# GpSimd makes three of four low parts in a projection, with a shorter routing, later waits for stores, and an output merged into the attention

## The chip, the cores and the metric

The kernel runs on one core of a Trainium2 chip. The metric is the device time of one execution in microseconds (us), the median over runs. Engine names: TensorE (PE in the rows, PEld for its weight loads), VectorE (DVE), ScalarE (ACT), GpSimd (POOL), SyncE (SP, which here only issues DMAs). A "q" behind an engine's name is its instruction queue.

## The reference

The input x has shape (2, 2048, 256). With `xn = layernorm(x)` over the last axis, the output is `x + attention(xn) + experts(xn)`:

```
qkv = xn @ Wqkv;  q, k, v of 16 heads of 16
q, k = rope(q), rope(k)                      # pairs of neighbours rotated by position
attn = softmax(causal(q @ k.T / 4));  attention = (attn @ v) @ Wout + bout

p = softmax(xn @ gate_w.T + gate_b)          # 10 gates: 8 experts and 2 null ones
weights, selected = top_k(p, 2)              # a null expert's weight is dropped, the rest rescaled
experts = sum over the selected e < 8 of  weight_e * (xn @ expert_w[e] + expert_b[e])
```

## The kernel before

The 4096 rows are 32 tiles of 128. The program has three blocks: `project`, `attend` and `output`. Between two blocks every engine waits until all engines have come to the end of the block. Within a block each engine has a list of instructions written out by hand, which it follows in order; semaphores tie them together. `wait_ge` stops the engine that meets it, and all that is queued behind.

**project** runs eight steps, s = 2j + b, each for 4 tiles (512 rows) of batch b. A step normalises rows (`norm_a` and `norm_c` on VectorE, `deviation` and `normal_x` on ScalarE, two steps ahead), turns them on TensorE (`transposes`), splits them in an fp16 high part (`high_x`, ScalarE) and low part (`low_x`, VectorE), and multiplies them by the weights: `queries` 0 to 3 give queries and keys transposed in psQ, `values` gives values and gate logits in psV. A product of split numbers is three fp16 products, high by high, high by low, low by high.

A query or key of index k (0 to 3) goes this way: `rope(s, k)` on VectorE (L559) multiplies psQ by cosines and sines into `turn[k]`; GpSimd combines two indices at once (L356 subtracts, L358 adds; `rot[k]` is the result); ScalarE writes the fp16 high part (`high`, L413, into `part[k]`); the low part `rot - high` is made by GpSimd for k = 0 and 2 (`low`, L345) and by VectorE for k = 1 and 3 (`split`, L564); and SyncE stores `part[k]` to memory (L250, semaphore `part_stored[k]`). `high(s, k)` waits until the store of step s-1 has landed, since it writes over the same tile. SyncE's order in a step is: normalised rows (L257), values (L245, once `copy_v` on ScalarE, L395, has filled `vst`), parts 0 to 3, and one expert's weights (L261), which `high_e` (ScalarE) and `low_e` (VectorE, L583) split, one expert a step.

Behind the steps comes the routing, almost all on VectorE (L633 to L700), each instruction waiting for the one before: add the gate bias, subtract the row's maximum, find the first and the second gate (`largest`, five instructions each), and write `sent`, which says for each row and expert whether the row goes there (L661). TensorE counts rows by expert (32 products, L771) and ranks them within each expert (33 products, L773 and L775). VectorE rounds the counts up to tiles of 128, a product sums them (L778), and VectorE works out each row's place `idx`, and `etab`, the expert of each of the 76 tiles (L695 to L700). ScalarE meanwhile issues the loads of the first group's keys and queries (L74), 24 DMAs. At the end SyncE waits for all stores and these loads.

**attend** goes through 8 groups of 4 heads in an order written out by hand. It begins with items for the first group (`first_items`): products of queries and keys (L1463, L1466) of which VectorE takes maxima (L1306). All semaphores of the block begin at one, which GpSimd sets, one instruction each, in the order in which they were made:

```python
for every in sems:
    pool.sem_inc(every, PV0 if every is pv_ok else ONE)
```

The expert products of 72 tiles run between the attention's, and behind the last group's scores TensorE does 7 and then 14 products that nobody reads (`idle_products`), and normalises the last outputs through psP.

**output** turns the attention's result for each of 32 tiles (L1673), copies it (ScalarE, L1694), multiplies it by Wout (L1684), adds the experts' part and the product to `acc` (VectorE, L1700 and L1704), and stores it.

## Time and profile before

| | us |
|---|---|
| median of 3 runs | 989.14 (989.03 to 990.25) |
| profiled execution, own time | 994.68 |
| its span (first to last instruction) | 993.0 |
| `project` | 0 to 133.5 |
| `attend` | 133.8 to 954.6 |
| `output` | 954.9 to 993.0 |

Over the span TensorE is busy 902.7 us (91%), VectorE 837.9 (84%), ScalarE 737.8 (74%), GpSimd 463.2 (47%), and the mean granted clock is 0.969. Busy time is a mean over stages with different limits; each stage must be read by itself. A row of the order of time gives start, duration, engine, line, operation, written tile and read tiles, shapes and, in brackets, how long the engine had been idle and what released it. Where a row merges several instructions (x2), its duration is that from the first's start to the last's end.

### The profile page before, as it was taken

Reading aid. Unit: us, or ns where it says so; the run is one execution under the profiler, and the core shown is the slowest. Engines: PE = TensorE matmul, PEld = TensorE weight load, DVE = VectorE, ACT = ScalarE, POOL = GpSimd, SP = SyncE. Lnnn points to the kernel's source line nnn. Section 1 sums busy time; section 2 is a strip of 40 time slices with the busy share of each in tenths; the row PEclk is TensorE's granted clock in tenths of the full one; section 3 lists DMA queues with packets and bytes.
Section 4 is the critical chain, followed back from the end, with each engine's and each line's share of the span. In section 5 each row is a group of like instructions: output and inputs, shape, how many; then the busy total and the mean of one; then the engine's idle time right before and its main releaser. Section 6 shows DMA issues by size and latency. Waiting matters only on the chain. (4 is left out here: it accounts for less than half of the span.)

```text
span 993.0 us, 22231 instructions
## 1 busy us (share of the span) xinstructions
PE 902.7 (91%) x7911; PEld 395.2 (40%) x7911; DVE 837.9 (84%) x1112; ACT 737.8 (74%) x1556; POOL 463.2 (47%) x588
## 2 busy tenths in 40 slices
PE   2888457999999999999999999999999999999888
PEld 1544233232432344444443544353444333322267
DVE  5999879999899978987889788978888899894856
ACT  3566323788788888888888789878887888789822
POOL 4677748585200353344834574355142344355620
PEclk9999775999999999999999999999999999999989
DMA  9777820301200424345414542265334321122113
GB/s 323 265 257 252 281 73 22 97 3 41 68 2 2 118 81 124 87 131 149 129 55 117 151 147 69 77 170 139 66 90 126 97 59 50 34 58 67 39 53 128
DMA packets 82133, 106.65 MB, mean 107 GB/s; under 512 B 10048, under 2 KB 59112, under 8 KB 81000
## 3 DMA queue, kind: packets, MB, share of 16 engines
q1 hardware_dynamic: 74536, 85.83, 27.2%
q0 software_dynamic: 6528, 17.83, 7.3%
q10 hardware_dynamic: 960, 1.57, 0.5%
q8 instruction: 64, 1.05, 0.4%
q14 instruction: 45, 0.37, 0.1%
HBM read 67.37 MB, written 37.50 MB: 106 GB/s over the span
## 5 line engine op out<-in xcount | busy, mean ns | idle before, releaser
L1306 DVE TENSOR_REDUCE blk<-psP 128x2 f32<-128x1024 f32 (+2 forms) x560 | 623.1, 1159 | 91.4 <-PE psP L1466 46.6
L1239 ACT ACTIVATE probs<-psS 128x512 f32<-128x512 f32 (+3 forms) x1280 | 588.0, 540 | 101.8 <-PE psS L1521 96.0
L1521 PE MATMUL psS<-Qs,Ks 50*128 50x512 f16 (+3 forms) x1280 | 329.1, 352 | 11.5 <-ACT probs L1239 7.0
L1463 PE MATMUL psP<-Ks,Qs 48*128 48x512 f16 (+2 forms) x1264 | 294.3, 359 | 22.6 <-DVE blk L1306 9.1
L1583 PE MATMUL psO<-probs,Vs 128*32 128x512 f32 (+3 forms) x2560 | 299.3, 545 | 6.0 <-POOL probs L1139 4.9
L1139 POOL TENSOR_SCALAR_AFFINE_SELECT probs<-probs 128x512 f32<-128x512 f32 x128 | 88.3, 690 | 337.6 <-ACT probs L1239 301.3
L1521 PEld LDWEIGHTS psS<-Qs,Ks 50*128 50x128 f16 x1280 | 96.0, 93 | 240.5 <-ACT probs L1239 155.2
L1463 PEld LDWEIGHTS psP<-Ks,Qs 48*128 48x128 f16 x1264 | 79.9, 94 | 119.6 <-DVE blk L1306 77.1
L1466 PE MATMUL psP<-later,eye 64*128 64x128 bf16 x1024 | 103.7, 222 | 0.0
L1583 PEld LDWEIGHTS psO<-probs,Vs 128*32 128x32 f32 x2560 | 52.8, 108 | 85.8 <-issue 65.1
L1466 PEld LDWEIGHTS psP<-later,eye 64*128 64x128 bf16 x1024 | 78.5, 99 | 19.9 <-issue 2.2
L1161 POOL DMA_INDIRECT xn<-norm_scratch,ids x72 | 69.4, 964 | 20.6 <-issue 8.1
L1556 PE MATMUL psS<-xn 128*128 128x256 f16 x432 | 57.0, 272 | 2.1 <-DMA xn<-be_scratch 0.8
L717 PE MATMUL psQ<-xp,wqp 128*128 128x512 f16 x192 | 47.6, 395 | 10.5 <-DVE turn L559 5.9
L1153 POOL TENSOR_SCALAR xn<-lane,at 128x128 f16<-128x128 f32 x64 | 39.7, 621 | 36.6 <-issue 19.6
L1556 PEld LDWEIGHTS psS<-xn 128*128 128x128 f16 x432 | 39.7, 97 | 18.1 <-issue 12.2
L1148 POOL DMA_INDIRECT xn<-expert_scratch,idx x32 | 30.3, 946 | 28.6 <-ACT probs L1239 25.9
L1173 POOL TENSOR_TENSOR xn<-xn 128x512 f16<-128x512 f32 x36 | 41.7, 1157 | 3.0
L1260 ACT COPY xn<-psS 128x512 f32<-128x512 f32 x36 | 21.1, 586 | 27.2 <-PE psS L1558 27.2
L1156 POOL TENSOR_SCALAR xn<-lane,at,number 128x76 f16<-128x76 f32 x64 | 40.6, 634 | 0.0
L559 DVE TENSOR_TENSOR turn<-psQ,trig 128x1024 f32<-128x1024 f32 x32 | 38.4, 1218 | 2.6 <-DVE part L564 1.8
L1256 ACT COPY xn<-psS 128x1024 f16<-128x1024 f16 x36 | 37.1, 1032 | 1.3 <-PE psS L1540 0.7
(186 smaller groups left out, 770.2 us busy)
## 6 DMA issues: line engine op xcount, KB each, us to landing
xn<-we_scratch SPq DMA_DIRECT2D x72, 256.0 KB
expert_scratch<-xn SPq DMA_DIRECT2D x36, 256.0 KB, 3.4
v_scratch<-vst SPq DMA_DIRECT2D x8, 1024.0 KB, 4.0
qk_scratch<-part SPq DMA_DIRECT2D x32, 256.0 KB, 4.0
Vs<-v_scratch SPq DMA_DIRECT2D x16, 512.0 KB, 3.9
Qs<-qk_scratch SPq DMA_DIRECT2D x168, 32.0 KB
Ks<-qk_scratch SPq DMA_DIRECT2D x168, 32.0 KB
acc<-x SPq DMA_DIRECT2D x8, 512.0 KB, 9.4
```

Of the source, the lines that this page charges most:

```text
L717: ins = pe.matmul(out, lhs(x, w, k), rhs(x, w, k), start=(n == 0), stop=(n == len(todo) - 1))
L1139: nc.gpsimd.affine_select(out=v, in_=v, compare_op=ALU.is_ge, fill=0.0, base=0, pattern=[[0, HG], [1, P]], channel_multiplier=-1).then_inc ...
L1156: nc.gpsimd.tensor_scalar(at_tile[:, n, :], lane[:, 0:MTILES], at[:, 0, n:n + 1], number[:, t:t + 1], ALU.is_equal, ALU.mult).then_inc(lis ...
L1161: nc.gpsimd.indirect_dma_start(out=xt[n % 2][:, t, :], out_offset=None, in_=xd[:, :], in_offset=bass.IndirectOffsetOnAxis(ap=ids[:, 2 * n ...
L1173: nc.gpsimd.tensor_tensor(xs[n % 2][:, 1, :], rows, xs[n % 2][:, 0, :], ALU.subtract).then_inc(x_split, 1)
L1239: nc.scalar.activation(probs[u % NPR][:, h, q0:CH], psS[:, k % SB, q0:CH], ACT.Exp, scale=exp_scale).then_inc(s_read[k % SB], 1)
L1306: nc.vector.tensor_reduce(out, src, AX.X, ALU.max).then_inc(item_ok[slot], 1)
L1463: ins = pe.matmul(psP[:, slot, at:at + w], Qs[r][rows, qt // CT, p, t * P:(t + 1) * P], Ks[r][rows, kc, p, 0:w], start=True, stop=True)
L1466: ins = pe.matmul(psP[:, slot, at + w - P:at + w], eye[all_rows, i, :], later[all_rows, i, :], start=False, stop=True, skip_group_check=True)
L1521: pe.matmul(psS[:, k % SB, q0:CH], Ks[r][rows, kt // CT, p, kt % CT * P:(kt % CT + 1) * P], Qs[r][rows, c, p, q0:CH], start=True, stop=Tru ...
L1556: pe.matmul(psS[:, bank, t * D:(t + 1) * D], xT[buf][:, w0, at_k:at_k + P], wt[2 * buf + t][:, of:of + D], start=(n == 0), stop=False)
L1583: ins = pe.matmul(psO[h * VW:(h + 1) * VW, q0:CH], Vs[r][:, kt, h * VW:(h + 1) * VW], probs[u % NPR][:, h, q0:CH], start=(kt == 0), stop=e ...
```

## The change

In `project`, GpSimd makes the low part of index 1 as well in each step; in the last step it makes all four, and the low parts of the last two experts. ScalarE no longer does `high` of index 2 and 3 at the start of the next step but in its own, behind `normal_x`. VectorE's `norm_a` and `low_e` move within the step. In the last step TensorE does `values` ahead of `queries` 2 and 3. The routing has fewer and smaller instructions: the first gate is found from the already subtracted maximum, counting goes by blocks of four tiles, counts are summed on VectorE, and `etab` is worked out as one column of 128 partitions and turned by a trip through memory. The waits for the last step's stores move into `attend`, and the buffers that these stores read lie where `attend` has `Qs[1]` and `Ks[1]`, which it writes only behind these waits. GpSimd sets `item_ok` first. `output` is merged into `attend`, without a block's end between them, in the same PSUM tiles, and the idle products are gone. The queries of the first group are loaded by SyncE instead of ScalarE.

```diff
+                if s == LAST:
+
+                    for k in range(QKT):
+                        sp.wait_ge(part_stored[k], ONE + 16 * LAST)
+                    load_heads(sp, qk_s, Qs[0], 0, Q_PARTS, slice(0, CHUNKS), 0, ahead_in)
                 for k in range(QKT):
                     sp.wait_ge(split_ok[k], ONE + s + 1)
...
-                    sp.wait_ge(el_ok, ONE + e + 1)
-                    sp.dma_start(we_s[e], wep[e % 2][:, :, :, :].rearrange("p w k n -> p (w k n)")
-                                 ).then_inc(e_stored[e % 2], 16)
+                    for late in {LAST - 1: (), LAST: (LAST - 1, LAST)}.get(e, (e,)):
+                        sp.wait_ge(el_ok, ONE + late + 1)
+                        sp.dma_start(we_s[late], wep[late % 2][:, :, :, :].rearrange("p w k n -> p (w k n)")
+                                     ).then_inc(e_stored[late % 2], 16)
+            sp.wait_ge(be_ok, ONE + 1)
+            sp.dma_start(be_s.rearrange("e p d -> e (p d)"), be_p[:, :, :].rearrange("e p d -> e (p d)")).then_inc(be_stored, 16)
             for b in range(2):
                 sp.wait_ge(v_stored[b], ONE + 16 * CHUNKS)
-                sp.wait_ge(e_stored[b], ONE + 16 * EXPERTS // 2)
-            for k in range(QKT):
-                sp.wait_ge(part_stored[k], ONE + 16 * NB * CHUNKS)
-            sp.wait_ge(be_ok, ONE + 1)
-            sp.dma_start(be_s.rearrange("e p d -> e (p d)"), be_p[:, :, :].rearrange("e p d -> e (p d)")).then_inc(spare, 16)
             sp.wait_ge(ahead_in, ONE + 16 * 2 * LOADS)
...
                         low(s, k0)
+                        if k0 == 0 or s == LAST:
+                            low(s, k0 + 1)
+                        if s == LAST:
+                            low_e(LAST - 1 + k0 // 2)
+
+            def low_e(e):
+                pool.wait_ge(eh_ok, ONE + e + 1)
+                nc.gpsimd.tensor_tensor(wep[e % 2][:, 1, :, :], we_sb[:, :, e * D:(e + 1) * D], wep[e % 2][:, 0, :, :],
+                                        ALU.subtract).then_inc(el_ok, 1)
...
+                ins = nc.scalar.activation(wep[e % 2][:, 0, :, :], we_sb[:, :, e * D:(e + 1) * D], ACT.Copy,
+                                           scale=wscale[:, OF_E:OF_E + 1])
+                if e >= LAST - 1:
+
+                    ins.then_inc(whole_ok, 1)
+                    act.wait_ge(whole_ok, ONE + e - LAST + 2)
+                    ins = nc.scalar.activation(we_sb[:, :, e * D:(e + 1) * D], we_sb[:, :, e * D:(e + 1) * D], ACT.Copy,
+                                               scale=wscale[:, OF_E:OF_E + 1])
+                ins.then_inc(eh_ok, 1)
...
-                    if not first:
-                        high(s - 1, 2)
-                        high(s - 1, 3)
                     if more:
                         high_x(s + 1, 1 - b)
                     high(s, 0)
                     if not last:
                         deviation(s + 2, b)
                     high(s, 1)
-                    copy_v(s, j, b)
                     if not last:
                         normal_x(s + 2, j + 1, b)
-                    high_e(s)
+                    if more:
+                        high(s, 2)
+                        copy_v(s, j, b)
+                        high(s, 3)
+                        high_e(s)
+                    else:
+                        copy_v(s, j, b)
+                        high_e(s)
+                        high(s, 2)
+                        high(s, 3)
 
             for j in range(CHUNKS):
                 body(j, j == 0, j == CHUNKS - 1)
-            high(LAST, 2)
-            high(LAST, 3)
             act.wait_ge(gate_in, ONE + 1)
...
                     rope(s, j, 1)
                     if not first:
                         split(s - 1, 3)
+                    if not last and not first:
+                        dve.wait_ge(x_in[s + 2], 16)
+                        norm_a(s + 2, j + 1, b)
                     if first:
                         scale_e()
                     if more:
                         low_x(s + 1, 1 - b)
                     rope(s, j, 2)
-                    if not first:
-                        low_e(s - 1)
-                    if not last:
+                    if first:
                         dve.wait_ge(x_in[s + 2], 16)
                         norm_a(s + 2, j + 1, b)
-                    rope(s, j, 3)
+                        rope(s, j, 3)
                     if not last:
                         norm_c(s + 2, b)
-                    split(s, 1)
+                    if not first:
+                        rope(s, j, 3)
+                        if s < LAST:
+                            low_e(s - 1)
...
-            low_e(LAST)
...
-            split(LAST, 3)
...
+            step(nc.vector.scalar_tensor_tensor(out=hot[0][:, :, :], in0=lg[:, :, :], scalar=0.0, in1=row(lower[:, :]),
+                                                op0=ALU.is_ge, op1=ALU.mult))
+            stepped()
+            foremost(hot[0][:, :, :])
...
+            dve.wait_ge(sent_ok, ONE + 1)
+            with nc.allow_low_precision(reason="counts up to 32 are whole numbers"):
+                nc.vector.tensor_reduce(some[:, :, :], sent[:, 0:TILES, :].rearrange("p (b t) e -> p b e t", t=BLOCK), AX.X,
+                                        ALU.add).then_inc(blocks_ok, 1)
+                dve.wait_ge(blocks_ok, ONE + 1)
+                nc.vector.tensor_reduce(total[:, :], some[:, :, :].rearrange("p b e -> p e b"), AX.X, ALU.add
+                                        ).then_inc(blocks_ok, 1)
+            none = (gm, gr)
+            for i in range(2):
+                step(nc.vector.tensor_tensor(none[i][:, :], hot[i][:, :, EXPERTS], hot[i][:, :, EXPERTS + 1], ALU.add))
+
             dve.wait_ge(count_ps, ONE + 1)
...
+            step(nc.vector.tensor_copy(countf[:, :], count[:, :]))
+            stepped()
+            step(nc.vector.tensor_tensor(shares[:, :, :], upto[:, :, :, :].rearrange("p i e f -> p (i e) f"),
+                                         countf[:, :].unsqueeze(1).to_broadcast([P, 2 * EXPERTS, EXPERTS]), ALU.mult))
+            stepped()
+            step(nc.vector.tensor_reduce(first[:, :, :].rearrange("p i e -> p (i e)"), shares[:, :, :], AX.X, ALU.add))
...
+            step(nc.vector.tensor_scalar(past[:, :], first[:, 1, :], row0[:, 0:1], None, ALU.is_le))
+            stepped()
+            step(nc.vector.tensor_reduce(number_past[:, :], past[:, :], AX.X, ALU.add))
+            stepped()
+            step(nc.vector.tensor_scalar_min(eplace[:, :], number_past[:, :], float(EXPERTS - 1)))
...
+                    if s == LAST:
+                        values(s, b)
...
+            pe.matmul(rank, upper[:, :], flat[:, 0:width], start=True, stop=True)
+            for t in range(1, BLOCK):
+                pe.matmul(inside[:, :, t * EXPERTS:BLOCK * EXPERTS], full[:, :], blocks[:, :, 0:(BLOCK - t) * EXPERTS],
+                          start=False, stop=True, skip_group_check=True)
+            pe.wait_ge(blocks_ok, ONE + 2)
+            pe.matmul(psV[:, 1, 0:EXPERTS], full[:, :], total[:, :], start=True, stop=True).then_inc(count_ps, 1)
+            for n in range(1, BLOCKS):
+                ins = pe.matmul(rank[:, n * BLOCK * EXPERTS:width].rearrange("p (b t e) -> p b t e", t=BLOCK, e=EXPERTS), full[:, :],
+                                some[:, 0:BLOCKS - n, :].unsqueeze(2).to_broadcast([P, BLOCKS - n, BLOCK, EXPERTS]),
+                                start=False, stop=True, skip_group_check=True)
+            ins.then_inc(ahead_ps, 1)
...
+            rows_of_ones(0)
             load_v(0, 0, 0)
             load_v(0, 0, 1)
+            for k in range(QKT):
+                sp.wait_ge(part_stored[k], ONE + 16 * B * CHUNKS)
+            for b in range(2):
+                sp.wait_ge(e_stored[b], ONE + 16 * EXPERTS // 2)
+            sp.wait_ge(be_stored, ONE + 16)
+            rows_of_ones(1)
+            sp.dma_start(et_s, eplace[0:MTILES, :]).then_inc(et_out, 16)
             n = first_items.index(("m", 1, 3))
             store_m(n % 2, n // 2, 0, 0, 3)
             load(1, 1, 1)
             load(1, 1, 0)
+            sp.wait_ge(et_out, 16)
+            sp.dma_start(etab[:, :], et_s.rearrange("n o -> o n")).then_inc(et_in, 16)
             sp.dma_start(wo[:, :, :], wout.rearrange("(k p) n -> p k n", p=P)).then_inc(wo_in, 16)
...
-            for every in sems:
+            for every in item_ok + [x for x in sems if x not in item_ok]:
...
+            for t in range(TILES):
+                act.wait_ge(t_ps, t + 1)
+                if t >= 2:
+
+                    act.wait_ge(o_ps, t - 1)
+                nc.scalar.copy(aT[t % 2][:, :, :].rearrange("p k n -> p (k n)"), psS[:, t % SB, 0:D]).then_inc(t_ok, 1)
...
+            dve.wait_ge(y_in[1], 16 * TILES)
+            dve.wait_ge(added, ONE + TILES)
+            for t in range(TILES):
+
+                nc.vector.scalar_tensor_tensor(out=acc[:, t, :], in0=second(t), scalar=wsel[:, 1, t:t + 1],
+                                               in1=acc[:, t, :], op0=ALU.mult, op1=ALU.add).then_inc(y_add, 1)
+                dve.wait_ge(o_ps, t + 1)
+                dve.wait_ge(y_add, t + 1)
+                nc.vector.tensor_tensor(acc[:, t, :], out_place(t), acc[:, t, :], ALU.add).then_inc(o_add, 1)
...
-                                idle_products(7)
+                                turn_out(0)
+                                turn_out(1)
...
-            idle_products(14)
...
+            pe.wait_ge(wo_in, ONE + 16)
             for t in range(TILES):
-                if t + 1 < TILES:
-                    turn(t + 1)
+                if t + 2 < TILES:
+                    turn_out(t + 2)
                 pe.wait_ge(t_ok, t + 1)
-                if t >= 4:
+                if t in (0, 2):
+                    slot = out_slot(t)
+                    pe.wait_ge(item_ok[slot], ONE + (ITEMS - slot + 1) // 2)
+                elif t >= 4:
                     pe.wait_ge(o_add, t - 3)
                 for k in range(KC):
-                    ins = pe.matmul(ps[:, t % 4, 0:D], aT[t % 2][:, k, :], wo[:, k, :], start=(k == 0), stop=(k == KC - 1))
+                    ins = pe.matmul(out_place(t), aT[t % 2][:, k, :], wo[:, k, :], start=(k == 0), stop=(k == KC - 1))
                 ins.then_inc(o_ps, 1)
```

## Rows read from the trace of the kernel before

**Rows 1.** Table of stretches: us, busy us of each engine (instructions), granted clock, DMA share, GB/s.

```profile
60.00:80.00 20.00, 16.70 (x106) 10.06 (x105) 19.55 (x37) 11.30 (x25) 14.53 (x11) 1.00 0.72 256
...
200.00:940.00 740.00, 720.15 (x6731) 289.51 (x6729) 631.69 (x732) 624.95 (x1326) 324.11 (x416) 1.00 0.30 85
```

**Rows 2.** VectorE in order of time, one step of the projection (s = 3).

```profile
59.27 2.35 DVE L559 TENSOR_TENSOR turn<-psQ,trig 128x1024 f32<-128x1024 f32 x2 [0.25 <-DVE part L564]
...
64.76 0.74 DVE L583 SCALAR_TENSOR_TENSOR wep<-we_sb,wscale,wep 128x512 f16<-128x512 f32 x1
...
68.63 1.79 DVE L564 TENSOR_TENSOR part<-turn,part 128x512 f16<-128x512 f32 x1
70.67 2.36 DVE L559 TENSOR_TENSOR turn<-psQ,trig 128x1024 f32<-128x1024 f32 x2 [0.25 <-DVE part L564]
```

**Rows 3.** GpSimd in order of time, same step.

```profile
68.60 1.27 POOL L356 TENSOR_TENSOR turn<-turn 128x512 f32<-128x512 f32 x1 [2.09 <-DVE turn L559]
...
72.21 1.16 POOL L345 TENSOR_TENSOR part<-turn,part 128x512 f16<-128x512 f32 x1 [0.66 <-ACT part L413]
```

**Rows 4.** ScalarE and SyncE in order of time; last, the view of line L250.

```profile
33.67 1.07 ACT L395 ACTIVATE vst<-psV 128x512 f32<-128x512 f32 x2
...
63.66 0.62 ACT L413 CAST part<-turn 128x512 f16<-128x512 f32 x1 [1.45 <-POOL turn L356]
...
67.89 1.08 ACT L395 ACTIVATE vst<-psV 128x512 f32<-128x512 f32 x2
...
68.99 0.33 SPq L245 DMA_DIRECT2D v_scratch<-vst  x1
69.37 4.94 SPq L250 DMA_DIRECT2D qk_scratch<-part  x4
...
106.85 0.62 ACT L413 CAST part<-turn 128x512 f16<-128x512 f32 x1 [2.38 <-DMA qk_scratch<-part]
...
DMA to landing us min/median/max: 2.2/4.0/5.4
```

**Rows 5.** Order of time, routing; last, SyncE's waits of 98 to 175 us.

```profile
109.36 0.20 ACT L398 ACTIVATE lg<-psV 128x40 f32<-128x40 f32 x1
...
111.71 1.54 DVE L633 TENSOR_TENSOR lg<-lg,gb_sb 128x320 f32<-128x320 f32 x1
...
115.36 5.62 ACTq L74 DMA_DIRECT2D Ks<-qk_scratch  x11
...
118.54 0.49 DVE L656 SCALAR_TENSOR_TENSOR gq<-hot,lg 128x320 f32<-128x320 f32 x1
...
121.68 0.43 DVE L661 TENSOR_TENSOR sent<-hot 128x256 bf16<-128x256 f32 x1
...
125.54 0.28 DVE L665 TENSOR_SCALAR count<-psV 8x128 uint32<-8x128 f32 x1 [3.44 <-PE psV L771]
...
127.96 0.42 DVE L677 TENSOR_TENSOR lg<-psV,first 128x256 f32<-128x256 f32 x1
...
131.53 0.78 DVE L695 TENSOR_TENSOR past<-first,row 128x608 f32<-128x608 f32 x1
...
133.17 0.20 DVE L700 TENSOR_SCALAR etab<-row 128x76 uint32<-128x76 f32 x1
...
SPq L84 <- DMA Qs<-qk_scratch: 3.4, 1, 3.4
```

**Rows 6.** The attention's first instructions in order of time; last, a stretch.

```profile
136.26 0.29 PE L1463 MATMUL psP<-Ks,Qs 48*128 48x128 f16 x1 [8.55 <-POOLq L1133]
...
137.32 0.69 DVE L1306 TENSOR_REDUCE blk<-psP 128x4 f32<-128x512 f32 x1 [2.33 <-PE psP L1466]
...
172.00:176.00 4.00, 4.00 (x29) 1.58 (x27) 1.95 (x3) 2.02 (x4) 2.26 (x4) 0.50 0.29 79
```

**Rows 7.** VectorE and TensorE in order of time, at the output's begin.

```profile
953.62 0.42 DVE L1329 TENSOR_TENSOR on<-psP,rs 128x256 f32<-128x256 f32 x1
...
955.80 1.13 PE L1684 MATMUL ps<-wo,aT 128*128 128x256 f32 x4 [0.24 <-ACT aT L1694]
```

189 lines of the change are left out of this document (76 added, 113 removed).

## The prediction

> **What bounds the kernel now.** I read the table of stretches first. The attention stage, 200 to 940 us, has TensorE busy 720 of 740 us, and no line of its loops changes. The projection (60 to 80 us) has VectorE busy 19.55 of 20 us, TensorE 16.7, GpSimd 14.5, and DMA at 0.72 of its capacity [rows 1]. So I look for gains at three seams: the projection with its routing tail (up to 133.4 us), the first microseconds of the attention, and the output.
>
> VectorE's order of time shows one step of the projection: the first rotation starts at 59.27 and that of the next step at 70.67, a pitch of 11.40, with 0.25 idle in it [rows 2]. VectorE sets the pitch, and the low part of index 1 at its end (68.63) takes 1.79.
>
> **The low part that moves.** With it VectorE loses everything from 68.63 to 70.67, 2.04 us, and its own work is 9.36 a step [rows 2]. The row is mostly waiting: GpSimd's sum starts at 68.60 and takes 1.27, and the low part ends about 0.55 after that [rows 2, 3]. GpSimd pays 1.16 for the same low part [rows 3], and goes to some 8.6 us a step with four sums at 1.27 and three low parts: no bound by itself. [...]
>
> **The new loop.** ScalarE now does the third high part and the value copy behind the four normalisations. The value copy (L395) therefore ends late, SyncE issues the value store after it, and the stores of the four parts stand behind that store in one queue. The high part of index 0 of the next step waits for its store to land. Before there was slack (at 63.66 ScalarE had waited 1.45 us for GpSimd), except once, at 106.85, where it had waited 2.38 us for that landing [rows 4]. The loop, by rows: value store issued at 68.99, just behind the copy, first part's store at 69.37, landing 4.0 later (the median), so 4.4 from the copy's end; high part 0.62; two low parts on GpSimd 2.3; one sum 1.27; high part of index 2, 0.62; value copy 1.08 [rows 3, 4]. That is 10.3. [...] The deviation, and the rotation behind it, also hang on that high part. [...]
>
> **Where that leaves the logits.** In step 0 the value copy ended at 34.7 [rows 4]; behind 2.07 of normalising and a high part with its sum it ends at about 37.9. Steps 1 to 5 at 10.9 bring it to 92.4, where five at 11.4 brought it to 91.8. Before, the two last steps were short, as they have nothing to normalise; now they still hang on the store: copy 6 at 103.3; then landing 4.7, two high parts 1.3, copy 1.1, logits 0.2: 110.7. Before, the logits were copied at 109.56 [rows 5]. They come 1.1 late, but VectorE no longer has the two last expert low parts and adds the bias at 110.7 and not at 111.71. So eight steps of a lighter VectorE are worth 1.0 us.
>
> **Routing, first part.** From 111.71 to the end of L661 at 122.11 are 10.40 us [rows 5]. Gone are the low part of index 3 (0.6) and two gate instructions; an undisturbed one has a pitch of 0.52 (118.54 and its 0.49 [rows 5]): 1.7 less. Against this, GpSimd still has some seven long instructions to do (a low part, two sums, two low parts, two expert low parts), where it had about three. Each VectorE instruction with two SBUF inputs may wait for the one under way: the first one did, 1.54 instead of 0.5 [rows 5]. Bounds: nothing, or 1.2 for each of six; I take 0.6 each, 3.6, since half of an instruction is the mean wait. The sent table then ends at 110.7 + 10.4 - 1.7 + 3.6 = 123.0.
>
> **Routing, the rest.** From 122.11 to 127.96 were 5.85: VectorE waited 3.44 for 32 counting products, converted, and waited for a product behind 32 others [rows 5]. Now: two sums over tiles (0.45 and 0.25), one product (0.25), three small instructions (0.2 each), a product and a sum of 128 elements (0.3 each): 2.4 with the hops. These sizes are not in the trace; the bounds are 1.8 and 3.2 by the 0.2 of L700 and the 0.42 of L677 [rows 5]. The seven block products (896 columns) run under them: the 32 narrow ones before, some 4,200 columns, took about 2 us. From 127.96 to 133.37 were 5.41; the table of experts (131.53 to 133.17, 1.64 for two instructions on 608 elements) falls to 0.4, and two additions leave: 1.5 less, 3.9. VectorE ends the projection at 123.0 + 2.4 + 3.9 = 129.3 in place of 133.4: minus 4.1.
>
> **Does anything else hold the exit?** The waits for stores of the last step move into the attention. SyncE still waits for the first head loads. ScalarE's first 12 stood at 114.79 to 120.98 and the other 12 behind them, with 3.4 of waiting for the landing [rows 5]. Now SyncE issues the query half before the last parts' stores, and ScalarE the key half after its last high part. I put that at 118 and the exponential at 119.5; 5.7 of issuing and 3.4 of landing end at 128.6. Hidden, but by 0.7 only: a faster routing would be held there.
>
> **The attention's first item.** TensorE's first product starts at 136.26, held by GpSimd's counters, of which the one it needs is about the thirtieth; VectorE's first maximum waits 2.33 and starts at 137.32 [rows 6]. With that counter first, TensorE is done by the time VectorE's own counter, then the thirtieth, is raised: 136.3. Minus 1.05. From there to 163 VectorE is the full engine, so its earlier start carries through. [...] The expert table's trip through memory is two small transfers on SyncE's queue, some 1 us before a store that comes behind 24 loads and for which nobody waits at once; nothing.
>
> **Output.** The last normalisation ends at 954.04 and the one before it 0.62 earlier, at 953.42; the first output product starts at 955.80, behind 14 idle products, the exit and one transpose with its copy [rows 7]. Now transposes and copies of the first tiles run while VectorE normalises: first product at 953.46, and one tile's transposes (0.22) fewer behind it. Minus 2.55. TensorE still does 32 tiles of 1.09, so nothing more comes out of it.
>
> **Sum.** 4.1 + 1.05 + 2.55 = 7.7. The profiled execution took 994.68 for a span of 993.0, and would take 987.0; the median of the three runs, 989.14, is 5.5 below the profiled one, and I take the same difference from it: 981.4.
>
> **Rivals.**
> A, the store loop is worse than the step it replaces: for it speaks the wait at 106.85 [rows 4], against it a DMA share of 0.72 [rows 1], under 0.8 at the new pitch. With a landing of 5.4 instead of 4.4 the step is 11.9: six steps give 6 us back, 987.4; if only half of the landings are that late, 984.5.
> B, the loop is looser (expert low part never in the way, landing hidden): pitch 9.9, six steps 6 us sooner, and the loads shift with them: 975.5. For it speaks that VectorE's work is 9.36; against it the single queue.
> C, routing is stretched by GpSimd as far as it can be: every one of six waits 1.2, as at 68.63 [rows 2, 3]: 3.6 more, 985. [...] At the other end no contention at all is 3.6 less, but the key loads hold 2.9 of it: 980.7.
> D, slower: the same queue, with the value store so late that each step costs more than 12.5. Then 6 x 1.6 = 9.6 eats all 7.7 and the 2 us of a measurement. [...] At 13 a step: 6 x 2.1 = 12.6, less 7.7, gives 994.
> E, no change: the attention gives back what the stages ahead of it gain, by a later rise of its clock: 988 to 990. Against it: the output's part lies behind the attention.
>
> **Numbers.** The forecast, 978.5 to 984, has 0.50; A 0.17; B 0.17; C (the stretched end) 0.07; D 0.04; E 0.05. A measurement of this kernel tells a change of about 0.2%, 2 us, from none. Faster by more than that needs less than 987.2: the forecast, B, C and most of A, 0.90; the same 0.06; slower 0.04. The range that leaves out 0.2 reaches half of B and most of A: 974.5 to 986.8.
>
> **What would show it.** The pitch of the first rotation (11.40) between 10.3 and 11.2; ScalarE's high part of index 0 released by a DMA in each step, and not by GpSimd; low parts of VectorE only for index 3; the write of `sent` ending near 123, with instructions of 0.8 to 1.5 among those with two inputs; exit at 129.3; the first maximum 2.4 after the attention's begin instead of 3.5; output products 0.04 after the normalisation. I am wrong if the pitch is 9.4 or above 11.4, if the key loads end the stage, or if the clock's rise, at 176 before, moves by more than the stages do.

## The result: no gain, and 0.2% lost

The changed kernel took 992.02 us (median of 14 runs, 987.51 to 994.08); the kernel before, run beside it, 989.58 (14 runs, 988.63 to 991.33). The ratio is 1.0021, 95% interval 1.0012 to 1.0031. Forecast were 981.4, with 974.5 to 986.8 as the range and 0.04 for slower.

The profiled execution took 994.08 for a span of 992.3. The table of stretches of the changed kernel, beside [rows 1]:

```profile
60.00:80.00 20.00, 16.64 (x98) 10.30 (x97) 15.67 (x33) 12.03 (x26) 14.84 (x12) 0.91 0.76 274
200.00:940.00 740.00, 718.85 (x6726) 290.21 (x6722) 628.47 (x721) 621.78 (x1318) 320.43 (x416) 1.00 0.30 85
```

VectorE is busy 15.67 of 20 us, no longer 19.55: the work did leave it. The steps didn't get shorter for it. The granted clock is 0.91 and no longer 1.00: it is at its lower level, 0.50, from 71.3 to 74.7 us, behind 3.3 us in which TensorE was busy for 1.04.

What holds a step stands in ScalarE's, GpSimd's and SyncE's order of time, one step of the changed kernel and the begin of the next (compare [rows 2 to 4]). In the changed kernel L250 is the value store, L260 the part stores, L430 `high` and L353 `low`:

```profile
85.19 0.33 SPq L250 DMA_DIRECT2D v_scratch<-vst  x1
85.56 4.34 SPq L260 DMA_DIRECT2D qk_scratch<-part  x4
...
91.72 0.62 ACT L430 CAST part<-turn 128x512 f16<-128x512 f32 x1 [4.38 <-DMA qk_scratch<-part]
...
92.41 2.27 POOL L353 TENSOR_TENSOR part<-turn,part 128x512 f16<-128x512 f32 x2 [3.57 <-ACT part L430]
...
98.17 0.33 SPq L250 DMA_DIRECT2D v_scratch<-vst  x1
98.54 4.01 SPq L260 DMA_DIRECT2D qk_scratch<-part  x4
...
102.97 0.62 ACT L430 CAST part<-turn 128x512 f16<-128x512 f32 x1 [2.65 <-DMA qk_scratch<-part]
```

The loop is the forecast one: value store (85.19), landing of part 0, high part of index 0 (91.72), and 6.45 later the next value store (98.17). Its landing wasn't the 4.4 of the forecast: from value store to high part are 6.53 in this step and 4.80 in the next (98.17 to 102.97). The view of waits from 24 to 117 us sums it up:

```profile
ACT part L430 <- DMA qk_scratch<-part: 22.0, 8, 4.4
POOL part L353 <- ACT part L430: 18.5, 9, 3.6
```

In each of the seven steps after the first, ScalarE waits for the landing of part 0 (the eighth wait of the row, 0.16, is for part 1); the kernel before did so once [rows 4]. The first rotation of the steps starts at 25.95, 35.43, 47.22, 58.54, 71.04, 82.31, 95.30 and 106.46; before, at 25.78, 36.45, 47.88, 59.27, 70.67, 82.08, 93.48 and 101.79. From 47.22 on the pitch is 11.2 to 11.3 and 12.5 to 13.0 in turns. In five of the seven steps high part 0 starts 4.8 after the value store's issue, in two later: 6.05 (at 67.46) and 6.53 (at 91.72).

The end of the projection in order of time, with the queues of SyncE and ScalarE (L74 are the first head loads), answers to [rows 5, 6]:

```profile
116.81 6.12 SPq L74 DMA_DIRECT2D Qs<-qk_scratch  x12
117.50 0.84 DVE L662 TENSOR_TENSOR lg<-lg,gb_sb 128x320 f32<-128x320 f32 x1
...
122.96 3.41 ACTq L74 DMA_DIRECT2D Ks<-qk_scratch  x9
122.97 2.01 SPq L260 DMA_DIRECT2D qk_scratch<-part  x4
...
127.42 0.50 DVE L692 TENSOR_TENSOR sent<-hot 128x256 bf16<-128x256 f32 x1
...
134.31 0.15 DVE L742 TENSOR_SCALAR eplace<-number_past 128x1 uint32<-128x1 f32 x1
138.95 0.48 DVE L1420 MEMSET ones<- 128x512 f16 x1 [4.49 <-PEq L84]
...
141.05 2.69 DVE L1393 TENSOR_REDUCE blk<-psP 128x4 f32<-128x512 f32 x3 [0.95 <-POOLq L1213]
```

and this is the line of SyncE's waits there:

```profile
SPq L278 <- DMA Ks<-qk_scratch: 8.1, 1, 8.1
```

Routing starts 5.8 late (117.50, before 111.71), but VectorE ends only 1.1 late (134.46, before 133.37). Then it stands for 4.49, because SyncE waits for the head loads: their last issue ends at 126.37, and the attention begins at 138.95, where the kernel before began at 133.83.

### The profile page after: what moved, and what is told of

It reads as the page before. It is cut to its first block, busy times and chain, and to the rows that moved or that the text cites. A ratio compares the mean times of both kernels' runs of the same rounds, so it can differ in the third digit from the quotient of the medians.

```text
span 992.3 us, 22081 instructions
## 1 busy us (share of the span) xinstructions
PE 901.6 (91%) x7836; PEld 393.1 (40%) x7836; DVE 826.4 (83%) x1102; ACT 740.1 (75%) x1558; POOL 465.0 (47%) x599
## 3 DMA queue, kind: packets, MB, share of 16 engines
q8 instruction: 64, 1.05, 0.4%
## 4 chain that ended last, share of the span: by engine, by line
PE 56%; DVE 19%; ACT 5%; issue 3%; POOL 2%; DMA 1%; SPq 1%; POOLq 0%; ACTq 0%; DVEq 0%
PE psO L1683 20%; DVE blk L1393 15%; PE psS L1618 13%; PE psP L1560 8%; ACT probs L1319 5%; PE psS L1653 4%; PE psP L1563 3%; PE psP L1752 3%; PE psS L1637 2%; DVE acc L1501 1%; PE psP L1733 1%; DVE xn L1401 1%; DMA xn<-be_scratch 1%; PE psS L1655 1%; PE psS L1664 1%
## 5 line engine op out<-in xcount | busy, mean ns | idle before, releaser
L1219 POOL TENSOR_SCALAR_AFFINE_SELECT probs<-probs 128x512 f32<-128x512 f32 x128 | 82.0, 641 | 341.2 <-ACT probs L1319 305.0
L430 ACT CAST part<-turn 128x512 f16<-128x512 f32 x32 | 19.8, 617 | 33.4 <-DMA qk_scratch<-part 22.0
```

The lines of the kernel that those rows point to most:

```text
L1219: nc.gpsimd.affine_select(out=v, in_=v, compare_op=ALU.is_ge, fill=0.0, base=0, pattern=[[0, HG], [1, P]], channel_multiplier=-1).then_inc ...
```

## Experiments

Each is the changed kernel with the edit shown, if it isn't said otherwise. The kernels g, k, l, m, n, p and q also have two lines near the end of the program, called the pauses here and told in the last part of this section; m and q are therefore read beside k, the changed kernel with the pauses alone, and n and p beside g. "Third memset" is the write of `nmp`, 0.72 after the attention's first instruction on VectorE; where an expectation speaks of the first memset with 128.6 or 139.7, it is this third one. Times from the traces, us:

```
kernel                         routing begins  VectorE's last  third memset
before                              111.71         133.17         134.55
changed kernel                      117.50         134.31         139.67
a, order undone                     111.88         127.27         132.38
b, order alone                      118.05         141.01         142.39
c, parts 0 and 1 first              108.30         124.76         128.56
d, key loads ahead                  117.22         133.76         145.03
g, c with the pauses                108.22         124.67         129.61
k, changed with the pauses          116.59         134.07         139.76
m, values copied early              111.94         129.42         135.62
n, c and m together                 105.78         123.26         129.16
q, queries loaded early             116.32         133.79         135.13
p, n and early queries              105.76         123.23         126.13
```

**Which half costs?** a_order_undone gives the old order back to the four engines:

```diff
-                        if k0 == 0 or s == LAST:
-                            low(s, k0 + 1)
...
+                    if not first:
+                        high(s - 1, 2)
+                        high(s - 1, 3)
...
+                    split(s, 1)
```

> The changed kernel with the projection's order of work put back to that of the kernel before (GpSimd makes low parts 0 and 2, VectorE 1 and 3, ScalarE makes high parts 2 and 3 at the next step's begin, values after queries in the last step); the routing, the stores' waits and the merged output stay. Theory 1 (the new order lost the time): the steps are 11.4 us again, the routing begins near 111.7 (changed kernel 117.50) and takes the changed kernel's 17.0 us, so VectorE is done near 129; the key loads, issued from 115 on, land by about 130; the attention's begin is near 130 where the kernel before had 133.8 and the changed one 138.95. With 1.4 us from the first item and 1.3 from the output that is 989.6 - 4.1 - 2.7 = 983 us (981 to 986). Rival 1 (the loads end the stage wherever VectorE is): the begin stays at 133.8, 987 us. Rival 2 (the order is innocent, the waits moved into the attention or the merged output cost it): 991 to 993 us.

Measured: 982.06, ratio 0.9925 (0.9901 to 0.9949). b_order_alone puts the new order, and nothing else, into the kernel before (the same lines with signs changed).

> The kernel before with only the new order of the projection (three low parts on GpSimd, ScalarE's new order, VectorE's new order, values ahead of the last queries, the last expert low parts on GpSimd); routing, waits and output are those of the kernel before. Theory 1 (the new order's loop through the value store and the landing of part 0 sets the step at 11.3 and 12.5 to 13 us in turns): routing begins 5.8 us late, at 117.5, and everything after it is as late: 989.6 + 5.8 = 995.4 us (993.5 to 997). Rival (the steps are longer only together with the moved waits or loads): 989 to 991 us.

Measured: 996.34, ratio 1.0067 (1.0040 to 1.0095). So the order costs 7.1 us and the rest gains 7.2: theory 1 both times, by the totals. Inside a, VectorE was done earlier than expected (127.4 for 129) and the attention began later (third memset 132.38 for some 130): it lies 5.1 behind VectorE's last instruction, not 1.4 as before. That is the loads' part, below.

**Is it the landing?** c_parts_first moves two stores in one queue:

```diff
+                store_parts((0, 1))
                 sp.wait_ge(v_ok, ONE + 2 * s + 2)
                 sp.dma_start(v_s[...], vst[b]...)
...
-                for k in range(QKT):
+                store_parts((2, 3))
```

> The changed kernel, but SyncE issues the stores of parts 0 and 1 of a step ahead of its value store (they are ready some 4 to 5 us before the values are copied). Theory 1 (the step is the loop value copy, stores, landing of part 0, next high part 0): the landing lies beside the value copy, ScalarE's 22 us of waits for the landing of part go, the step comes to 10.4 to 11.2 us (VectorE is busy for 10.3 of it), the routing begins near 110.5 to 112, VectorE ends near 128, the key loads some 4 us behind it, near 132: 992.0 - 6.5 = 985.5 us (983 to 988). Rival 1 (the DMA queues' throughput holds the step: 2 MB a step leave in one burst): the wait moves to another store, steps near 12, 991 to 993 us. Rival 2 (GpSimd's longer sums and low parts hold it): steps 11.4 to 12, 989 to 992 us.

Measured: 981.92, ratio 0.9916 (0.9888 to 0.9945). No run lies near that median: four took 977.92 to 979.56, four 984.27 to 985.99 (two groups of runs, told below). With the pauses, which leave one group, it is 979.64 (g) against 991.41 (k): 11.8 us less. That is more than the 4 to 9 us expected. The table of stretches, and from the view of waits, what is left of the landing's up to 100 us:

```profile
60.00:80.00 20.00, 16.98 (x106) 10.04 (x105) 17.89 (x36) 13.29 (x29) 17.10 (x14) 1.00 0.75 268
```

```profile
ACT part L434 <- DMA qk_scratch<-part: 1.1, 1, 1.1
```

The engines do the same work in the same order as in the changed kernel; only the place of two stores differs. The rotations come every 10.76 us (35.41 to 89.23, five steps), the clock is 1.00 again, and routing starts 9.2 earlier. The same bytes go out in 1.1 us less a step, so throughput didn't hold the step of the changed kernel. i_old_order_parts_first is the control, the same edit under the old order:

> The changed kernel with the projection's old order of work (as in a_order_undone), and parts 0 and 1 stored ahead of the values. A control. Theory 1 (the part stores' place matters only in the new order, where the high part of the next step waits for their landing): VectorE sets the step at 11.40 us as before and nothing changes against a_order_undone: 981 to 983 us in the lower group of runs. Rival (the earlier stores help any order, through less crowded queues): 978 to 980 us.

Measured: 987.66 (985.65 to 988.63; all its runs are of the upper of the two groups), and not the 981 to 983 expected of the lower one. Group for group it is the same: profiled span 986.6 where a_order_undone, also in its upper group, had 986.2, routing at 111.89 as against 111.88. No effect: the stores' place matters only where something waits for it.

m_copy_early attacks the other leg of the loop, in the changed kernel (with the pauses):

```diff
+                    if more:
+                        copy_v(s, j, b)
                     if not last:
                         normal_x(s + 2, j + 1, b)
                     if more:
                         high(s, 2)
-                        copy_v(s, j, b)
```

> The changed kernel (with the pauses), but ScalarE copies the values directly behind high part 1, as in the kernel before, ahead of the rows' normalisation and of high part 2. The part stores stay behind the value store. Theory 1 (the loop is: landing of part 0, high part 0, value copy, value store, part stores): from the release of high part 0 to the value store 3 us instead of 6.5, with the landing's 4.8 to 6.5 some 8 to 9.5 us, under VectorE's 10.3 busy us a step, so the step is 10.5 to 10.9 us and the begin of the routing 108 to 110: 979 to 982 us. Rival 1 (the queues hold the step, whatever the copy's place): 12 us steps, as k_after_gaps. Rival 2 (values copied early delay the rows' normalisation, and TensorE waits for the transposes): steps of 11.2 to 12 us, 984 to 990 us.

Measured: 988.55, ratio 0.9994 (0.9986 to 1.0003), 2.9 less than k_after_gaps. The step is 11.5 us: theory 1 is out, and so is the 12 of rival 1. It is the size of rival 2, but not for its reason: from 42 to 95 us TensorE waited only 1.2 us for normalised rows. The order of time shows another one:

```profile
53.46 0.62 ACT L430 CAST part<-turn 128x512 f16<-128x512 f32 x1 [2.85 <-DMA qk_scratch<-part]
...
54.70 1.07 ACT L412 ACTIVATE vst<-psV 128x512 f32<-128x512 f32 x2
...
57.55 0.43 SPq L267 DMA_DIRECT2D norm_scratch<-xn  x1
58.03 0.57 SPq L250 DMA_DIRECT2D v_scratch<-vst  x1
...
58.64 5.27 SPq L260 DMA_DIRECT2D qk_scratch<-part  x4
...
66.08 0.62 ACT L430 CAST part<-turn 128x512 f16<-128x512 f32 x1 [4.35 <-DMA qk_scratch<-part]
```

The values are copied by 55.8, but their store stands in SyncE's queue behind the store of the normalised rows (57.55), which waits for ScalarE's normalisation. So the value store is issued 4.57 after the high part instead of 6.45. With that 512 KB just ahead of it, part 0 is free 8.05 after it in this step and 6.2 to 6.6 in the steps between, where the changed kernel had 6.1 to 6.5 and 4.8. Most of what was won at one end of the loop was lost at the other. n_parts_first_copy_early has both edits:

> Both: parts 0 and 1 stored ahead of the values, and the values copied directly behind high part 1 (with the pauses). Theory 1: the loop is off the path already with one of the two, VectorE's chain sets 10.5 us a step, nothing is gained over g_gaps: 978 to 980 us. Rival (the loop still held a part of the step in g_gaps): steps of 10.3 us or less, 976.5 to 978 us.

Measured: 980.37, ratio 0.9909 (0.9896 to 0.9922), beside 979.64 for g_gaps (c with the pauses, below). Routing started 2.4 earlier than there (105.78, 108.22), and the attention 0.4 (129.16, 129.61). The steps had got shorter and the time hadn't, and that leads to the loads.

**The loads' end.** d_keys_ahead issues the key loads before ScalarE's last two high parts:

```diff
                         high_e(s)
+                        for k in range(QKT):
+                            act.wait_ge(part_stored[k], ONE + 16 * LAST)
+                        load_heads(act, qk_s, Ks[0], 1, K_PARTS, ...)
                         high(s, 2)
```

> The changed kernel, but ScalarE issues the twelve key loads ahead of its last two high parts, not behind the exponential: from about 117.8 us on where the changed kernel had 121.1 to 126.4, and so ahead of the last step's part stores (issued from 123.0) and the last two expert stores. Theory 1 (the key loads end the stage because they lie behind 1.5 MB of stores in the DMA engines): the loads land before VectorE is done at 134.5, the attention begins near 135 instead of 138.95: 992.0 - 3.9 = 988.1 us (987 to 989.5); the exponential is some 4 us later, near 126, and VectorE waits for it only from 128 on. Rival (the transfers share their rate whatever the order): the last load lands near 138 again, 991.5 to 992.5 us.

Measured: 1001.07, ratio 1.0094 (1.0063 to 1.0125), 9 us above the changed kernel. Not all of the 9 is the edit's: the profiled run has the slow mask told below (7.20 us), as five of the six runs seem to, and the sixth took 995.0. The edit's own part stands at the attention's begin, 5.4 later than in the changed kernel (145.03, 139.67), and that is the wrong way. Order of time, and the view of the part stores' line from 117 us on:

```profile
117.56 5.89 SPq L74 DMA_DIRECT2D Qs<-qk_scratch  x12
117.89 5.77 ACTq L74 DMA_DIRECT2D Ks<-qk_scratch  x12
123.50 5.60 SPq L260 DMA_DIRECT2D qk_scratch<-part  x4
129.14 7.43 SPq L272 DMA_DIRECT2D we_scratch<-wep  x2
136.62 0.88 SPq L275 DMA_DIRECT2D be_scratch<-be_p  x1
144.31 0.48 DVE L1420 MEMSET ones<- 128x512 f16 x1 [10.40 <-PEq L84]
```

```profile
DMA to landing us min/median/max: 19.3/20.3/20.9
```

With all 24 loads in the air together, the part stores behind them took 20 us to land, and SyncE needed 7.43 just to issue two expert stores. Between 121 and 127 us the queues moved 135 GB/s at a share of 0.67; the kernel before, whose loads followed one another on one queue, moved 174 at 0.53 over the same 6 us. The loads' 2 KB packets took some 0.18 us each here, 0.095 before and 0.13 in the changed kernel. So these packets are slower in the two kernels where two engines issue; whether that comes from the two queues or from the number of transfers in the air, these runs don't separate.

h_one_queue puts the query loads of c back behind the key loads on ScalarE:

```diff
-                    load_heads(sp, qk_s, Qs[0], 0, Q_PARTS, ...)
...
             load_heads(act, qk_s, Ks[0], 1, K_PARTS, ...)
+            load_heads(act, qk_s, Qs[0], 0, Q_PARTS, ...)
```

> The kernel with parts 0 and 1 stored first, but with the query loads issued by ScalarE behind the key loads, as the kernel before has it, not by SyncE beside them. Theory (query and key loads in the air at once slow each other: their 2 KB packets took 0.20 to 0.22 us each between 120 and 132 us of the changed kernel, 0.09 to 0.11 in the kernel before, whose 24 loads followed one another): the loads begin near 111.6 and are over 13.5 us later, as before (114.8 to 128.3), at about 125; VectorE, done at 124.8, ends the stage again and the attention's begin (first memset) moves from 128.6 to about 126.2: 2.4 us less than the kernel with parts first, some 976.5 to 978 us in its lower group of runs (that one's is 977.9 to 979.6). Rival (the issue of 24 loads on one engine takes 10 us and is as late as the crowd was): no change, 979 us.

Measured: 985.96, in the upper group; its profiled span is 982.4 where c's, in the same group, is 982.8, the third memset at 128.17 (c: 128.56). The packets did fall to 0.097, but the last ended at 126.1, as the issue of 24 loads had run to 122.9: the rival. f_queries_early is c with three of four chunks of the query loads behind the sixth step's stores:

```diff
+                    if e == LAST - 2:
...
+                        load_heads(sp, qk_s, Qs[0], 0, Q_PARTS, slice(0, CHUNKS - 1), 0, ahead_in)
```

> The kernel with parts 0 and 1 stored first, but three of four chunks of the first head group's query loads are issued by SyncE behind the stores of the sixth step (about 95 us), only the last chunk after the last value store; key loads as in the changed kernel. Theory (the loads' end, 3.8 us behind VectorE's, sets the attention's begin): most of the query bytes are in before the crowd, the rest is over by about 124, VectorE's end (124.8) sets the begin, 126.2 instead of 128.6: 2.4 us less, 976 to 977.5 us in the lower group. Rival (the loads of 6 us of issue on SyncE delay the sixth and seventh steps' stores, which delay ScalarE's high parts): the projection ends 1 to 4 us later and the gain is eaten, 978 to 982 us.

Measured: 984.48 (979.43 to 985.43). Its two lower runs took 979.4, as the lower ones of c did (977.92 to 979.56), and its profiled span is 983.0 beside 982.8: nothing won. The loads no longer held the exit (VectorE stood for 0.46), but a high part waited 3.72 for its landing at 106.87, routing began 1.0 later and VectorE ended 2.2 later: the rival again. q_after_queries_early moves them one step on, behind stores for which no later high part waits:

```diff
                     stores(e, j, b)
+                    if e == LAST - 1:
+                        for k in range(QKT):
+                            sp.wait_ge(part_stored[k], ONE + 16 * (LAST - 2))
+                        load_heads(sp, qk_s, Qs[0], 0, Q_PARTS, slice(0, CHUNKS - 1), 0, ahead_in)
```

> The changed kernel (with the pauses, to be read beside k_after_gaps), but three of four chunks of the query loads are issued by SyncE behind the seventh step's part stores, on which no later high part waits, and only the last chunk behind the last value store. Theory (the loads' end is the missing 4 us of the change's sum): the attention's begin (first memset) comes 1.4 to 2 us behind VectorE's end, near 135.5 to 136 instead of 139.7, and the kernel takes 987 to 988.5 us. Rival 1 (the loads are not what ends the stage): 991 us, begin near 139. Rival 2 (the loads crowd the eighth step's stores or VectorE's own end moves by as much): 989 to 991 us.

Measured: 987.23, ratio 0.9977 (0.9968 to 0.9985), 4.2 less than k_after_gaps. SyncE's wait, then VectorE's order of time:

```profile
SPq L282 <- DMA Ks<-qk_scratch: 1.0, 1, 1.0
```

```profile
133.79 0.15 DVE L746 TENSOR_SCALAR eplace<-number_past 128x1 uint32<-128x1 f32 x1
134.41 0.48 DVE L1424 MEMSET ones<- 128x512 f16 x1 [0.46 <-PEq L84]
```

The wait at the exit, 4.49 in the changed kernel and 4.82 in k_after_gaps, is 0.46, as before the change. p_best does the same in n:

> The kernel with parts 0 and 1 stored first and the values copied early (with the pauses; to be read beside n_parts_first_copy_early), and three of four chunks of the query loads issued by SyncE behind the seventh step's part stores. Theory (the loads' end is the floor of the stage: VectorE was done at 123.3, the begin came at 129.2): the begin comes at 124.7 to 126.5 and the kernel takes 976 to 978 us. Rival (something else holds the begin at 128 to 130 us in all these kernels): 980 us again.

Measured: 978.26, ratio 0.9887 (0.9872 to 0.9901), 2.1 less than n, with the third memset at 126.13. The begin is at the upper end of what was expected, the time 0.3 above it, and SyncE still waits 2.1 for a query load. It has the lowest median here, of four runs.

**Two groups of runs.** g_gaps is c with

```diff
+                    if t % 4 == 3:
+                        dve.wait_ge(added, ONE + t + 1)
```

in the loop of `add_first` (32 multiply-adds of VectorE, near the end), and l_before_gaps and k_after_gaps are the two kernels of the case with the same two lines.

> The kernel with parts 0 and 1 stored first, but VectorE's 32 multiply-adds of add_first near the end wait for their own completion after every fourth. In the profiles of the kernel before, of a_order_undone and of c_parts_first a mask of GpSimd took 7.2 us until VectorE's run of 32 was over, in those of the changed kernel and of b_order_alone the same mask, begun at the same point, took 0.85 us; and the runs of most kernels fall into two groups some 5.5 to 6 us apart (the kernel before: 988.4 to 990 and 994 to 995.5). Theory (whether the mask gets in is a coin toss, and it makes the two groups): with the pauses the mask gets in every time, the upper group is gone, all runs lie at 978 to 980 us. Rival 1 (the groups have another cause): both groups stay, 978 to 980 and 984 to 986 us. Rival 2 (the pauses make the run of 32 late for the output): all runs 1 to 2 us above the lower group.

> The kernel before with the pauses of g_gaps. Theory: the upper group of the kernel before (993.5 to 996) is gone, all runs lie at 988.5 to 990 us, and the mask that took 7.2 us takes under 1.5 us in the profile. Rival (the groups have another cause): some runs at 994 to 996 us.

> The changed kernel with the pauses of g_gaps in VectorE's 32 multiply-adds, and nothing else. It takes the coin toss near the end out of the comparison and gives a second profile of the change. Theory (the change gives routing's begin +5.8, routing -4.7, the loads' end +4.0, first item -1.4, output -2.7, and some runs a wait of some 2 us for the loads of the expert biases near 385 us with a stretch of lower clock behind it): 990 to 992 us, 1 to 2 us above l_before_gaps. Rival (the wait near 385 us is in every run of the change): 992 to 994 us, and it stands in this profile too.

The mask (a select of GpSimd over the softmax's tile), in order of time, in the kernel before:

```profile
931.74 13.50 DVE L1414 SCALAR_TENSOR_TENSOR acc<-xn,wsel,acc 128x256 f32<-128x256 f32 x32
...
938.55 7.18 POOL L1139 TENSOR_SCALAR_AFFINE_SELECT probs<-probs 128x512 f32<-128x512 f32 x1
```

the same one in the changed kernel:

```profile
945.68 0.85 POOL L1219 TENSOR_SCALAR_AFFINE_SELECT probs<-probs 128x512 f32<-128x512 f32 x1
```

and in g_gaps:

```profile
924.38 15.07 DVE L1505 SCALAR_TENSOR_TENSOR acc<-xn,wsel,acc 128x256 f32<-128x256 f32 x32
...
931.11 0.79 POOL L1223 TENSOR_SCALAR_AFFINE_SELECT probs<-probs 128x512 f32<-128x512 f32 x1
```

Measured: g 979.64 (978.77 to 982.55, 4 runs), l 990.55 (989.53 to 992.22, 11 runs), k 991.41 (988.70 to 994.78, 11 runs). Beside g, 10 of 11 runs of the kernel before lay between 993.5 and 996.1, and h and i, without the pauses, between 984.5 and 988.7; no run of g was above 982.6, and its mask took 0.79. That is why the ratio of g (0.9860) flatters it: the kernel before, beside it, was in its upper group. All seven profiles with a mask of 7.2 are of a run of the upper group, and the two without the pauses and with a mask of 0.85, those of the changed kernel and of b_order_alone, are not. So for g the theory held.

l and k prove less. The share of upper runs changes from one set of runs to the next: of the kernel before it was 0 of 14 beside the changed kernel, 4 of 19 beside a to d, 10 of 11 beside g, and 0 of 29 beside l and k. That l has no upper run shows nothing, since the kernel before had none beside it; that it pays 1.4 us for the pauses can be read. Of the change k says: 0.9 us over l, in the order of what the terms below give.

## Why the prediction was wrong

**The step's pitch** was forecast as 10.9: a loop of 10.3, with 4.4 from the copy's end to the landing, and 0.6 more, my estimate for VectorE's expert low part holding up GpSimd's sum in that loop. No run shows that 0.6; what they showed in its place is that sum at 1.62 beside the expert low part and not at 1.27, some 0.35 more. The loop was the right one, and the first of the two failures is its landing: "landing 4.0 later (the median)". From the value copies' ends (38.8, then 98.1 for step 5) the pitch is 11.87; the forecast had 37.9 and 92.4. The way from high part 0 to the next value store took 6.45, where 10.9 less 4.4 leaves 6.5: right. (The 0.35 is in it.) From the value store's issue to high part 0 the same five steps took 5.4 in the mean, where I had 4.4: that is all of the 1.0.

Two things are in it. The 4.0 was the median over the stores of all four parts. Part 0's own store, behind the values, had landed 4.3 to 4.6 after its issue in the first six steps of the kernel before, and landed after 4.3 to 4.4 in five of seven of the changed one: some 0.4 a step, and nothing new about the store. In the other two it took 5.6 and 6.1, and these cost 3.0 together. The kernel before had landings of 5.3 to 5.4 in its last two steps, and only one was waited for: while a store isn't on the path its late landings are hidden, and once it is each counts in full.

Rival A had the mechanism and its size, 11.9 at a landing of 5.4, with 0.17; rival D, over 12.5 in each step, is out by the mean of 11.87: landings near 6 came in two steps only. The logits were copied at 116.2 and routing began at 117.50: 6.8 late against 110.7. Of that 0.9 comes from step 0, 4.9 from the five steps, and 1.1 from the end, where VectorE was in its last two rotations (115.06 to 117.58) when the logits were there; from copy 5 to copy 6 it took 10.9 (10.9), from there to the logits 7.3 (7.4). c and n show that the loop is this one.

**Routing, first part**: 10.42 (117.50 to 127.92) where I had 12.3. GpSimd's contention was priced at 3.6, and that is what it came to: eight of VectorE's instructions with two SBUF inputs took 0.65 to 1.35 us instead of 0.49, 3.6 more in all, and the sums with one input took 0.48 to 0.49. The mistake is in what the 3.6 was added to. The 10.40 of the kernel before held 2.2 of the same contention (instructions of 1.54, 0.81, 0.64, 0.84 and 0.79), so it was counted twice. With that the forecast was 1.9 too slow here, which by luck made up for a part of the first failure. Rival C's stretched end, six waits of 1.2, is refuted.

**Routing, the rest**: 6.54 from `sent` to VectorE's end (134.46); 6.3 forecast, 11.26 before. Right.

**The exit** is the second failure: "3.4 of landing [...] Hidden, but by 0.7 only". From the end of the last key load's issue to the end of SyncE's wait it took some 12 (126.37 to about 138.3), since the key and query loads were in the air together and beside them 1.5 MB of stores. The 3.4 was the tail of 24 loads in a row, whose last stood alone. Price: 4.0 at the exit; q, which sends most query loads ahead, is 4.2 faster than k. Loads ending the stage had been named as a thing that makes the forecast wrong; it had no price and no chance.

**First item**: begin to first maximum 2.10, before 3.49: minus 1.4, forecast minus 1.05. Right.

**Output**: in the changed kernel the product stands 0.42 behind the end of a normalisation, its last one comes after the product, and the two traces are of different groups. a_order_undone is of the group of the kernel before; its order of time answers to [rows 7]:

```profile
948.64 0.42 DVE L1391 TENSOR_TENSOR on<-psP,rs 128x256 f32<-128x256 f32 x1
...
949.21 1.10 PE L1727 MATMUL psP<-wo,aT 128*128 128x256 f32 x4 [0.25 <-DVE on L1391]
949.26 0.42 DVE L1391 TENSOR_TENSOR on<-psP,rs 128x256 f32<-128x256 f32 x1
```

The product comes 0.15 behind the normalisation's end (948.64 and 0.42), 0.04 forecast; from the last normalisation's start to the end of the span are 36.9 us, before 39.4. Minus 2.4, forecast minus 2.55. Right.

**Sum.** Forecast minus 7.7. Misses: begin of routing 6.8, routing itself minus 1.6 (16.96 instead of 18.6), exit 4.0, first item minus 0.3, output 0.15: together 9.0, so plus 1.3. Measured were plus 2.4, and 0.9 between k and l. The rest may be a wait of some of the change's runs, which spread more (987.5 to 994.1) than those of the kernel before; the profiled one has it. Order of time, then the table of stretches:

```profile
385.37 1.44 PE L1653 MATMUL psS<-xn 128*128 128x256 f16 x6 [1.72 <-DMA xn<-be_scratch]
```

```profile
385.00:388.70 3.70, 3.33 (x18) 2.44 (x19) 0.00 (x0) 0.15 (x1) 0.04 (x1) 0.54 0.67 201
```

TensorE stands 1.72 for an expert's biases, and right behind it the granted clock is at its lower level, 0.50, for 3.4 us. Together they cost 3.5: the last normalisation to start ahead of them comes 3.8 behind the same one of the kernel before (357.60, 353.83), the next 7.3 (430.68, 423.42). k's profile has 0.2 of this wait, and no such stretch. What brings it on stays open. The two profiles agree with this sum: their spans are 992.3 and 993.0, but the kernel before is profiled in its upper group, so that like for like the changed one is 4.8 to 5.3 us longer: the 1.3 and these 3.5.

**The sign.** Rivals D and E, the only ones on the other side, held 0.09. Either failure alone, 6.8 or 4.0 of 7.7, would have left something of the gain. The first was a rival, weighed alone, the second half a sentence without a price; nothing stood for both at once. Rival E's 988 to 990 comes within some 2 us of the measured time, but it isn't what happened: the first maximum comes 3.7 later than before, a normalisation at 243.58 (before 239.81) 3.8 later, and the granted clock rises from 0.50 at 180.5 instead of 176.3. So the attention begins later and gives nothing back of it; there was no gain ahead of it to give back.

## What to carry to other kernels

A wait for a store to land is priced by what that very store took in the old trace, late ones included, not by a median over its neighbours: a late landing that slack used to hide counts in full once the store is on the path. If a store frees a buffer for which an engine waits, it goes ahead of the large one for which nobody waits (g against k: 11.8 us for two moved stores). A stretch taken over from the old trace already holds its own contention; only what is added to it may be charged. When a change takes the bounding engine's work away, list each stage's exit with all that ends there, and price the second as if it ended last: here the loads, 0.7 us behind on paper, took the gain of the routing. Two failures that act in series are added, not weighed against one another.

## What the runs showed of the hardware

A GpSimd mask that starts 6.81 us into a run of 32 VectorE multiply-adds with two SBUF inputs took 0.85 us in the changed kernel and 7.18 in the kernel before, there to 945.73, 0.49 behind the run's end (945.24). Groups of runs 5.5 to 6 us apart go with it, and g, where VectorE waits for itself after every fourth (mask 0.79), had no upper group. What decides between the two stays open, and so does what the two engines hold each other up by.

Two of the seven landings of part 0 in the changed kernel were 1.2 to 1.7 us later than the others. In each of those two windows one instruction packet of 16 KB, some 1 us of one DMA engine's time (0.8% of 16 over 8 us), lies between the value store and the landing; here from 84 to 92 us:

```profile
q8 instruction: 1, 0.02, 0.8%
```

and none from 74 to 80 us. (A third, at 38.4, begins just ahead of its value store, and that store landed 0.1 later than the others.) m's late landings (66.08, 89.48) have theirs too, and so have those of b_order_alone and k_after_gaps, where again two of seven value stores landed after 5.6 to 5.9 and the rest after 3.9 to 4.2. That this packet delays its engine's share of the store fits; no run puts it elsewhere to test it.

The value store and the four part stores together move 2 MB, from 74 to 80 us at 342 GB/s. Part 0, 256 KB, took 4.3 to 6.1 us to land in the changed kernel's first seven steps, where it is issued behind the 1 MB of the values. In c, where it is issued ahead of them, it took 3.5 to 3.8 in steps 1 to 6, and the values 5.0 to 6.9, where they took 4.0 to 5.8 in the same steps of the changed kernel.
